# Equality matrices made in place from key rows that go through memory, no barrier after the first layer, and the second layer's totals from its scaled matrix

## The reference, cut to what matters

```python
edge_index = stack([src, dst])
x = layernorm(x + L0(x, edge_index))                    # two SAGE convolutions
x = layernorm(x + L1(x, edge_weight, src, dst))         # ten similarity-weighted steps
x = layernorm(x + L2(x, src, dst))                      # attention over edges, then an FFN
x = layernorm(x + L3(x, edge_attr_4, edge_attr_32, dst, src))  # equivariant messages

# L0, one convolution
agg = segment_sum(x[src], dst) / maximum(count(dst), 1)
y   = agg @ W_l.T + b_l + x @ W_r.T

# L1
xn  = x * rsqrt(maximum(sum(x * x, 1), 1e-12))
sim = where(src == dst, 0, sum(xn[src] * xn[dst], -1))
s   = exp(sigma)
sup = edge_weight * exp(sim / (2 * (2 * s * s)))
denom = b + segment_sum(sup, src) * a + a               # a = exp(alpha), b = exp(beta)
for _ in range(10):
    out = (x * b + (segment_sum(sup * out[dst], src) + out) * a) / denom
```

## Time and profile before

| | |
|---|---|
| time, median of 3 runs | 2785.97 us (2780.97 to 2790.19) |
| the profiled execution's own time | 2781.79 us |
| its span in the profile | 2780.0 us, mean granted TensorE clock 0.898 |
| busy | PE 82%, DVE 65%, POOL 41%, ACT 36% |
| barrier after the first layer's edge work | ends near 1303 us |
| PE matmuls, whole program | 9582 |

### The profile page before, as it was taken

How to read it: one execution, slowest core, us unless ns; L and a number is a source line. 1 busy time by engine, 2 the same in 40 slices (tenths; PEclk the granted TensorE clock), 3 DMA queues, 4 the chain that set the end, 5 groups by cost and what they waited for, 6 DMA issues and landing times.

```text
span 2780.0 us, 28864 instructions
## 1 busy us (share of the span) xinstructions
PE 2290.1 (82%) x9582; PEld 1197.5 (43%) x9582; DVE 1806.6 (65%) x3856; ACT 1008.9 (36%) x1735; POOL 1135.8 (41%) x869
## 2 busy tenths in 40 slices
PE   8999999999999689996076766739998898389786
PEld 4455555555555345453031211214444553254465
DVE  7999888888878861445753433544567658557753
ACT  2354545454555432210432322321121132265553
POOL 2766654455675724301645665620210201233222
PEclk9999999999999889998587988869999697599898
DMA  7333443333343435325744645670210202222221
GB/s 245 99 103 105 118 121 120 104 118 108 108 111 104 129 95 167 104 76 165 206 139 134 175 131 155 153 222 10 67 48 27 73 1 74 75 71 69 57 57 53
DMA packets 214547, 298.62 MB, mean 107 GB/s; under 512 B 100006, under 2 KB 100501, under 8 KB 213018
## 3 DMA queue, kind: packets, MB, share of 16 engines
q1 hardware_dynamic: 108186, 213.98, 25.7%
q0 software_dynamic: 106240, 83.12, 12.1%
HBM read 171.66 MB, written 160.65 MB: 120 GB/s over the span
## 4 chain that ended last, share of the span: by engine, by line
PE 56%; DVE 20%; issue 7%; POOL 6%; DMA 5%; ACT 5%; SPq 1%; POOLq 0%; DVEq 0%; ACTq 0%
PE bank L2031 8%; PE bank L320 8%; PE bank L1010 7%; PE bank L304 5%; POOL arena L1624 4%; PE bank L2627 3%; PE bank L296 3%; PE bank L990 2%; PE bank L311 2%; DMA arena<-y_table,ids 2%; DVE st L642 2%; POOL arena L1102 2%; PE bank L312 2%; PE bank L2510 2%; DMA x_table<-arena 2%
## 5 line engine op out<-in xcount | busy, mean ns | idle before, releaser
L1102 POOL DMA_INDIRECT arena<-x_table,idd x120 | 152.0, 1267 | 648.2 <-DVE arena L2297 157.1
L1678 PE MATMUL bank<-arena 125*125 125x512 f32 x360 | 207.5, 709 | 108.6 <-DMA arena<-y_table,ids 103.7
L2031 PE MATMUL bank<-arena 128*125 128x512 f32 x640 | 293.7, 614 | 1.4 <-DVE Md L2251 0.7
L304 PE MATMUL bank<-arena 128*125 128x512 f32 x640 | 285.2, 599 | 8.6 <-DMA ident<-ident_in 8.6
L1624 POOL DMA_INDIRECT arena<-y_table,ids x180 | 229.6, 1276 | 153.1 <-DMA y_table<-arena 101.0
L320 PE MATMUL bank<-arena 128*125 128x512 f32 x640 | 278.5, 593 | 2.1 <-ACT arena L517 1.8
L1852 DVE SCALAR_TENSOR_TENSOR arena<-arena,v,bank 125x512 f32<-125x512 f32 x180 | 134.3, 746 | 188.1 <-PE bank L1678 180.0
L811 POOL TENSOR_TENSOR arena<-arena,rowv 125x512 f32<-125x512 f32 x80 | 99.5, 1278 | 315.4 <-DVE arena L725 201.7
L1018 ACT ACTIVATE arena<-bank 128x500 f32<-128x500 f32 (+1 forms) x210 | 114.6, 589 | 279.3 <-PE bank L962 145.4
L1010 PE MATMUL bank<-arena 128*125 128x512 f32 x480 | 208.8, 593 | 0.0
L1729 ACT ACTIVATE bank<-arena 125x512 f32<-125x512 f32 x180 | 107.6, 600 | 267.5 <-DVE arena L1852 262.4
(11 more groups left out here) (404 smaller groups left out, 4417.4 us busy)
## 6 DMA issues: line engine op xcount, KB each, us to landing
y_table<-arena SPq DMA_DIRECT2D x36, 896.0 KB
p_table<-arena SPq DMA_DIRECT2D x25, 896.0 KB
z_table<-arena SPq DMA_DIRECT2D x25, 896.0 KB
x_table<-arena SPq DMA_DIRECT2D x25, 896.0 KB
arena<-x_cols SPq DMA_DIRECT2D x20, 1000.0 KB, 6.4
arena<-x SPq DMA_DIRECT2D x20, 896.0 KB
out<-arena SPq DMA_DIRECT2D x20, 896.0 KB
x_by_src<-arena SPq DMA_DIRECT2D x5, 896.0 KB
```

The costliest lines, as they stand in the source:

```text
L304: i = nc.tensor.matmul(b[0:P, :], xT[:, k, j * P:(j + 1) * P], W1r[:, k, :], start=k == 0, stop=k == KC - 1)
L1102: nc.gpsimd.indirect_dma_start(out=dst, out_offset=None, in_=table, in_offset=bass.IndirectOffsetOnAxis(ap=idx, axis=0), bounds_check=limi ...
L1678: nc.tensor.matmul(bank[t % RING1][0:P, :], Ss[:, t, :], V1[:, t, :], start=False, stop=True, skip_group_check=True).then_inc(P_sum, 1)
L2031: i = nc.tensor.matmul(b[0:P, :], fT[:, k, j * P:(j + 1) * P], W[:, k, :], start=k == 0, stop=k == KC - 1)
```

## The change

1. The hardware loop ends two steps earlier (LOOP_END 12 instead of 14), so all work on the records is done two steps earlier: DVE's in step 12, the scatters in 12 to 15, their return on SP in 15, DVE's part of it in 16.
2. A new table `key_rows` in memory holds the dst keys and the src keys as two rows of 2,500 numbers. When the scatters have landed, SP copies the key column of each record table into it (two DMAs from memory to memory, elements of 4 bytes that lie 192 bytes apart in the source), waits for both, and then loads the first row onto all 125 partitions of `Sd`. Only then it issues the loads that it issued before.
3. DVE makes `Sd` and `Md` in place from those key rows, in two parts, in steps 17 and 18 (BUILDS0), and the boundary weights in step 18. ACT's diagonals, PE's L1252 and DVE's reads of them from PSUM are gone, in both layers. SP's small transfers after the build move from step 20 to step 19.
4. `Ss` is loaded in the same way by SP near the end of the first layer's edge work, and made in place by DVE at the second layer's start.
5. The barrier `end_phase` is gone, and POOL does not wait for the build of `Ss` between its first gathers.
6. The second layer's scalars are in another order: what does not need ACT comes first, and the wait for ACT's exponential of the three parameters is parted from the wait for its root. `Ss` is scaled first, and PE takes the totals from the scaled matrix times a column of ones, four matmuls ahead of each group of `first_own`; DVE computes its ratio per group.

The diff, its core:

```diff
-        LOOP_START, LOOP_END = 8, NG - 6
+        LOOP_START, LOOP_END = 8, NG - 8
...
-            if isinstance(s, int) and s == BUILD0:
-                pe.wait_ge(NR_sb, st_.count("b_f", 4))
-                pe_build(pe, c, diag0, 1)
...
-            if isinstance(s, int) and s == BUILD0 - 1:
-                act.wait_ge(rec_done, 2)
-                for t in range(ET):
-                    i = nc.scalar.activation(diag0(t // TG)[:, t % TG, :], ident[0:P, 0:P], ACT.Identity,
-                                             scale=RD[:, t, Q_DST:Q_DST + 1])
-                i.then_inc(s_end, 1)
...
+            if isinstance(s, int) and s in BUILDS0:
+                dve_build(dve, c, 0, RD[:, :, Q_DST], Sd, Md, *BUILDS0[s])
+            if isinstance(s, int) and s == NG - 2:
+                link(dve, c, nc.vector.reciprocal(v20[:, 8, :], RD[:, :, Q_CNT]))
+                dve_boundary_weights(dve, c, Bd[:, :], 0, RD[:, :, Q_DST], None, bn0)
             if has(s, "S"):
                 finish(C, "sc", "rt", "rc", nS, 3)
-            if isinstance(s, int) and s == ENDS0:
-                link(dve, c, nc.vector.reciprocal(v20[:, 8, :], RD[:, :, Q_CNT]))
-                dve_boundary_weights(dve, c, Bd[:, :], 0, RD[:, :, Q_DST], None, bn0)
...
+        key_rows = nc.dram_tensor("key_rows", (2, E), F32).ap()
...
-        def end_phase(eng, c):
-
-            eng.drain().then_inc(phase_end, 1)
-            c.ph += 1
-            eng.wait_ge(phase_end, 4 * c.ph)
...
+        BUILDS0 = {LOOP_END + 5: (0, 3), LOOP_END + 6: (3, EG)}
...
             sv = RSd.rearrange("(t p) q -> p t q", p=P)
+            with nc.allow_non_contiguous_dma(reason="the keys of sorted records as two rows"):
+                sp.dma_start(key_rows[0], RDd[:, Q_DST]).then_inc(rec_back, 16)
+                sp.dma_start(key_rows[1], RSd[:, Q_SRC]).then_inc(rec_back, 16)
+            sp.wait_ge(rec_back, 16 * 2)
+            sp.dma_start(Sd, key_rows[0].rearrange("(t f) -> t f", f=P).partition_broadcast(P)).then_inc(rec_back, 16)
             sp.dma_start(RD[:, :, :], dv).then_inc(rec_back, 16)
             sp.dma_start(rec[:, :, :], sv).then_inc(rec_back, 16)
...
-        def dve_build(dve, c, q, key, S, M, dg):
-
+        def dve_build(dve, c, q, key, S, M, g0, g1):
+
+            t = slice(g0 * TG, g1 * TG)
             dve.wait_ge(dstep, c.d)
-            if dg is not None:
-                nc.vector.tensor_tensor(dg[:, :, :], spread(ident[0:P, 0:P], ET), b3(key, P),
-                                        ALU.mult).then_inc(s_end, 1)
-            for g in range(EG):
-                kt = gcols(key, g)
-                dve.wait_ge(R_ps, c.r + 1)
-                b = bank[4 + c.r % RN]
-                c.r += 1
-                row = b[0:P, 0:GR].rearrange("p (t f) -> p t f", f=P)
-                nc.vector.tensor_tensor(S[0:P, g * TG:(g + 1) * TG, :], row, b3(kt, P), ALU.is_equal)
-                nc.vector.tensor_copy(gcols(ck[:, q, 0:ET], g), row[:, :, 0])
-                i = nc.vector.tensor_copy(gcols(ck[:, q, ET:NB], g), row[:, :, P - 1])
-                if M is None:
-                    i.then_inc(R_sb, 1)
-                    continue
-                nc.vector.tensor_tensor(M[:, g * TG:(g + 1) * TG, :],
-                                        b[0:NB, 0:GR].rearrange("p (t f) -> p t f", f=P),
-                                        b3(gcols(bkm[:, q, :], g), P), ALU.is_equal).then_inc(R_sb, 1)
-            dve.wait_ge(R_sb, c.r)
-            link(dve, c, nc.vector.tensor_tensor(many[:, q, :], ck[:, q, 0:ET], ck[:, q, ET:NB], ALU.not_equal))
+            if M is not None:
+                nc.vector.tensor_tensor(M[:, t, :], S[0:NB, t, :], b3(bkm[:, q, t], P), ALU.is_equal)
+            nc.vector.tensor_copy(ck[:, q, t], S[:, t, 0])
+            link(dve, c, nc.vector.tensor_copy(ck[:, q, ET + g0 * TG:ET + g1 * TG], S[:, t, P - 1]))
+            i = nc.vector.tensor_tensor(S[:, t, :], S[:, t, :], b3(key[:, t], P), ALU.is_equal)
+            if g1 == EG:
+                link(dve, c, i)
+                link(dve, c, nc.vector.tensor_tensor(many[:, q, :], ck[:, q, 0:ET], ck[:, q, ET:NB], ALU.not_equal))
...
+            sp.wait_ge(R_sb, jobs0_done("z", EG - 1))
+            sp.dma_start(Ss, key_rows[1].rearrange("(t f) -> t f", f=P).partition_broadcast(P)).then_inc(rec_back, 16)
...
-        totals = bank[4][0:P, 0:ET]
-        totals_rdy, TOT0 = s_end, 2
+        totals = [bank[4 + 2 * (g % 2)][0:P, TG * g:TG * (g + 1)] for g in range(EG)]
...
             targets(0)
-            pool.wait_ge(R_sb, c.r + EG)
...
+            def group_totals(g):
+                pe.wait_ge(w1_rdy, g + 1)
+                if g >= 2:
+                    pe.wait_ge(P_raw, TG * (g - 1))
+                for j in range(TG):
+                    q = nc.tensor.matmul(totals[g][:, j:j + 1], Ss[:, TG * g + j, :], ones[:, 0:1], start=j == 0,
+                                         stop=True, skip_group_check=True)
+                q.then_inc(totals_rdy, 1)
...
             for g in range(EG):
                 tiles = range(TG * g, TG * (g + 1))
+                group_totals(g)
...
-            dve_build(dve, c, 1, RSs[:, :, 1], Ss, None, diag1)
+            dve.wait_ge(rec_back, 16 * 10)
+            dve_build(dve, c, 1, RSs[:, :, 1], Ss, None, 0, EG)
...
             nc.vector.tensor_scalar_max(v20[:, 5:7, :], v20[:, 5:7, :], 1e-12).then_inc(sc1, 1)
-            dve.wait_ge(sc1a, 2)
+            link(dve, c, nc.vector.tensor_tensor(TMP, RSs[:, :, 0], RSs[:, :, 1], ALU.not_equal))
+            link(dve, c, nc.vector.tensor_tensor(SD, SD, TMP, ALU.mult))
+            sg = v20[:, 8, 0:1]
+            dve.wait_ge(sc1a, 1)
             link(dve, c, nc.vector.reciprocal(v20[:, 5:7, :], v20[:, 5:7, :]))
             link(dve, c, nc.vector.tensor_tensor(SD, SD, SSQ, ALU.mult))
             link(dve, c, nc.vector.tensor_tensor(SD, SD, DSQ, ALU.mult))
-            link(dve, c, nc.vector.tensor_tensor(TMP, RSs[:, :, 0], RSs[:, :, 1], ALU.not_equal))
-            link(dve, c, nc.vector.tensor_tensor(SD, SD, TMP, ALU.mult))
-            sg = v20[:, 8, 0:1]
+            dve.wait_ge(sc1a, 2)
             link(dve, c, nc.vector.tensor_tensor(sg, abv[:, 2:3], abv[:, 2:3], ALU.mult))
             link(dve, c, nc.vector.tensor_scalar_mul(sg, sg, 4.0))
             link(dve, c, nc.vector.reciprocal(sg, sg))
             nc.vector.tensor_scalar(SD, SD, sg, None, ALU.mult).then_inc(sc1, 1)
             dve.wait_ge(sc1a, 3)
             al, be, both = abv[:, 0:1], abv[:, 1:2], v20[:, 9, 0:1]
-            nc.vector.tensor_tensor(both, al, be, ALU.add)
...
-            nc.vector.tensor_tensor(SUP, SD, RSs[:, :, 2], ALU.mult).then_inc(sc1, 1)
-            dve.wait_ge(sc1, 3)
+            link(dve, c, nc.vector.tensor_tensor(SUP, SD, RSs[:, :, 2], ALU.mult))
+
+            def scaled(g):
+                Sg = Ss[:, g * TG:(g + 1) * TG, :]
+                nc.vector.tensor_tensor(Sg, Sg, b3(gcols(SUP, g), P), ALU.mult).then_inc(w1_rdy, 1)
+            scaled(0)
             nc.vector.tensor_tensor(BM[:, :, 0:NM], BM[:, :, 0:NM], b3(SUP, NM), ALU.mult).then_inc(bm_rdy, 1)
-            for g in range(EG):
-                Sg = Ss[:, g * TG:(g + 1) * TG, :]
-                dve.wait_ge(totals_rdy, TOT0 + g + 1)
-                nc.vector.tensor_tensor(Sg, Sg, b3(gcols(SUP, g), P), ALU.mult).then_inc(w1_rdy, 1)
+            link(dve, c, nc.vector.tensor_tensor(both, al, be, ALU.add))
+            for g in range(1, EG):
+                scaled(g)
...
-            ratio(RR, NRR, totals, P)
             for t in range(ET):
+                if t % TG == 0:
+                    dve.wait_ge(totals_rdy, TOT0 + t // TG + 1)
+                    ratio(gcols(RR, t // TG), gcols(NRR, t // TG), totals[t // TG], P)
...
+                if isinstance(s, int) and s == NG - 1:
+                    sp.wait_ge(bn0, 1)
```

More of the change, by code:

```diff
@@ L415, in pe_step @@
                 rows_T("c_x", X3[par], True)
-            if isinstance(s, int) and s == BUILD0:
-                pe.wait_ge(R_sb, EG)
             if isinstance(s, int) and s == ENDS0:
@@ L1120, in scatter @@
                                          oob_is_err=False).then_inc(s, 16)
-        BUILD0, ENDS0, FIRST0 = NG, NG + 1, NG + 2
-        def diag0(g):
-            return at(GR * g if g < 4 else 34249, [TG, P], P)
+        ENDS0, FIRST0 = NG + 1, NG + 2
+        BUILDS0 = {LOOP_END + 5: (0, 3), LOOP_END + 6: (3, EG)}
         ones = sb("ones", [P, P])
@@ L1278, in gnn_kernel @@
             + [("n", g) for g in range(EG)]
-        R0 = EG
+        R0 = 0
         def jobs0_done(kind, g):
@@ L1647, in first_own @@
                                  stop=True).then_inc(P_sum, 1)
-            pe.wait_ge(sc1, 3)
-            for t in range(ET):
-                q = nc.tensor.matmul(totals[:, t:t + 1], Ss[:, t, :], SUP[:, t:t + 1], start=t == 0, stop=True,
-                                     skip_group_check=True)
-                if t % TG == TG - 1:
```

(4 more changed lines are left out.)

38 lines of the change are left out of this document (6 added, 32 removed).

## The result

The changed kernel takes 2805.41 us (median of 6 runs, 2798.88 to 2809.35), the kernel before 2787.76 us (6 runs, 2780.55 to 2795.06). The ratio is 1.0076, with a 95% interval of 1.0056 to 1.0095. The time lies within the forecast range, near the upper end, but the kernel became slower where no change was forecast as the likeliest. The condition of the third rival came, copies that take over 18 us (they took 22.9), and a time near its 2806. Its mechanism, small writes that are slow, did not (experiment 10), and the parts of its sum are not those measured, so that the near hit is in part luck.

The account below looks back on a forecast made before the run. PE's program order was taken as the bound. Second layer -13, drain -3, builds +1 and SP's queue +14.3 gave -0.7 on 2781.79, about 2781, or 2785 on the runs' scale; 8-in-10 range 2769 to 2806 us.

Parts of the forecast that it names:

- third rival: Node loop, SP's queue: 4-byte copies go at the pace of small writes, 30 us for both, total 2806; chance 0.18.
- term for SP's queue: Node loop, records' return: key copies and `Sd` load delay what is queued behind them, +14.3 us, ends +2.9 and +35.
- the prediction's own sign: Node loop: the prediction is wrong if no step is longer, or if one is longer by over 20 us.
- the copies: SP's queue: both key copies take 9.2 us, from 5.7 for the record loads plus 3.5; bounds 3.5 and 30.
- the load: SP's queue: loading 1250 KB into `Sd` takes 9.5 us at 135 GB/s, or 3.8 at 335 GB/s.
- the slack: Node loop: 4.4 us between the result store's read of its tile ending and DVE overwriting that tile, subtracted from the loss.
- The sum: Whole kernel: second layer -13, drain -3, builds +1, SP's queue +14.3, together -0.7 us against the profiled execution.
- Second layer's start: Second layer up to its first products: -10 until the products end, -1 table load, -2 totals, together -13 us.
- The landing of the last gather: Second layer's start: the last gather lands in 4 to 5 us instead of 10.78, a gain of 6.
- Drain: Node loop's steps 20 and 21: -1.9 and -1.9 us, +0.8 for a lower PE clock, together -3.
- Builds: DVE in steps 17 and 18: builds cost between 0 and 8.8 us, taken as +1.
- Rival 4: Second layer's totals: small groups with waits leave PE's clock low, up to 20 us more, 2805; chance 0.07.

Follow-up runs that it names:

- experiment 10: Changed kernel, with the records loaded first and the dst keys written to the key row from the loaded tile, not copied in memory: 2801.99 us, one execution.
- experiment 1: Changed kernel, with the src keys' copy moved to the first layer's edge work, so one key copy stands ahead of the `Sd` load: 2799.32 us, one execution.
- experiment 9: Changed kernel, with the `Sd` load cut into two DMAs of 112 and 13 partitions and nothing else: 2808.39 us, one execution.
- Experiment 6: Transfers spread over steps 15 to 17, builds in 17 and 18, barrier after the first layer back: ratio 1.0005 to the kernel before, 0.9974 without the barrier.
- experiment 7: Transfers spread over steps 15 to 17, builds in 17 and 18, totals as before the change: ratio 0.9989 to the kernel before, 0.9974 with grouped totals.
- experiment 4: Changed kernel, with record return, dst copy and `Sd` load spread over steps 15 to 17, builds in 18 and 19, src copy late: 2773.13 us, ratio 0.9958.

## Why the prediction failed

**The loss: mechanism and place right, size wrong.** The step that failed is the term for SP's queue, +14.3, where 32.2 came; 17.9 too little. By the prediction's own sign, a step longer by over 20 us, it was wrong: step 16 is 23.8 longer. The 17.9 have three parts.

- 13.7 are the copies: 22.9 us instead of 9.2. I took 5.7 us for 2,500 pieces from the record loads, which go from memory to SBUF, and let two run side by side. They do run side by side (the second adds 6.5), but one alone takes 16.4 (experiment 1), and from SBUF 7.9 (experiment 10): the nearest row had another kind of source and destination. It was also not a transfer's time: the 5.59 us of the earlier trace rows are how long SP's queue was held. The second key copy held it for only 4.80, and landed 21.94 us after its issue. The upper bound of 30 us held; my reason against it, that 1.49 is POOL's pace and not the DMA's, was not tested.
- 2.2 are the load: 11.7 beyond what the records took, against 9.5 (its own row, 135 GB/s, gives 9.3 for 1.25 MB, and 335 GB/s gives 3.7); 5.7 of them go when it is cut (experiment 9).
- 2.0 are the slack: I subtracted 4.4, where 34.6 us of delay on SP made 32.2 of stall, so 2.4.

The wait that I had named, DVE's for the result's store, is there; PE's for its columns, 24.73 us, stands beside it and was not in my sum. That freeing the result's tile earlier would have gained little follows from it, but no run tried it.

**The sum.** With 22.9 for the copies alone it gives -0.7 + 13.7 = +13, with the measured stall in the place of the whole term -0.7 + 17.9 = +17. That this meets the 17.6 of the medians is luck in part: in the two profiles the places that were forecast give 32.9 - 5.7 - 13.2 = +14.0, and the rest of their difference is elsewhere. The direction hung on one unknown price: the copies' bounds were 3.5 and 30 us, and I had taken 9.2, in the lowest quarter.

**Second layer's start: right in sum, one part by luck.** -13 forecast, -13.2 measured in this pair. The three profiles of the kernel before have 132.3 to 134.6 us for this stretch and ten with the change 121.3 to 124.4, so the gain is more nearly 10, with 8 and 13 as ends. By its parts, from the end of the first layer: first gather -2.6 (forecast -3.2), last gather's issue -7.9 (-7.8), products' end -9.3 (-10), start of the totals -9.9 (-11, or -10.4 with the scaling ahead of them), first products' end -13.2 (-13). The landing of the last gather failed: it gained 1.6 us and not 6, since its 9.15 us are near the 10.78 of before. The 4 us that I had taken off for squares and products hid that, so the -10 was right for a wrong reason. On PE the totals were to bring -2.6 to +0.6 (its own terms give -2.8). Experiment 6 gives 4 to 5 of the gain to the barrier, experiment 7 0.4 to 2 to the totals; the rest, the in-place build, POOL's freedom from it and the order of the scalars, was not undone alone.

**Drain: -5.7 in this pair against -3, and hardly told from nothing.** The two other profiles of the kernel before have 367.7 and 368.4 us for this stretch, the first 371.4; ten with the builds in steps 17 and 18 have 364.9 to 369.4. So the gain is some 2 us on the average, and the rest of the 5.7 is what two executions differ. In this pair PE's L296 of step 20 comes 2.7 us nearer to the last z store, the rest later; the 0.8 for a lower clock did not come (0.84 after, 0.80 before).

**Builds: right.** Step 19 is 0.7 longer than 45.5, step 18 not at all; +1 was forecast. Step 17 lies in the stall and can't be read. In experiment 4 no step shows them.

**Rival 4, the clock, did not come:** 1.00 from 1417 on, 6 us behind the first total.

**Not forecast: +6.2 at the start**, with the same instructions. See the last section; the cause stays open.

## What to carry to other kernels

A DMA that costs no engine anything still costs what is queued behind it: before adding one, list the transfers behind it on its queue and when their users want them, and put it where the queue has nothing urgent for as long as it runs. Here the same transfers cost 32 us in one step, and over three steps 4, or nothing with the builds a step later. Price a copy by the landing of one with the same source, destination and piece size, not by how long its issue held the queue; if there is none, the sign of a change that depends on it is open, and the forecast should say so. Two things are worth trying: to take small pieces from SBUF (7.9 us against 16.4 here), and to cut a load over 125 partitions in 112 and 13 (5.7 us sooner in its place). Neither showed in a time by itself. And before a difference of a few us in one pair of profiles is explained, look at the same stretch in a second profile of the same kernel: here the drain's 5.7 shrank to some 2.

## What the runs showed of the hardware

A copy of 2,500 elements of 4 bytes, 192 bytes apart, from memory to memory takes 14.8 to 16.4 us alone from its issue to that of the load that waits for it, a second one beside it 6.5 more; from SBUF 7.9 us.

In the first 50 us POOL's work slows DVE's. DVE counts keys in instructions of 0.35 us; when POOL runs 125 x 512 additions beside them, they take 1.23 to 1.45, as long as one addition (1.26). Changed kernel, DVE and POOL:

```profile
44.67 0.35 DVE L470 SCALAR_TENSOR_TENSOR Bd<-Md,kfc,ones 125x125 uint8<-125x125 f32 x1
...
46.53 1.23 DVE L470 SCALAR_TENSOR_TENSOR Bd<-Md,kfc,ones 125x125 uint8<-125x125 f32 x1
```

```profile
45.07 1.26 POOL L787 TENSOR_TENSOR arena<-arena,rowv 125x512 f32<-125x512 f32 x1 [13.66 <-DMA arena<-x]
```

In the first profile of the kernel before that addition starts at 46.98, 1.9 us later, and only one of the last DVE instructions meets it: 5 slow ones in all there, 6 in its second profile, 8 in each of twelve profiles with the change. That is the first 2.6 us of the 6.2. The start follows from the landing of a load of rows, whose instructions are the same. Three profiles without the change have the sixth z store at 257.8 to 260.4, twelve with it at 261.8 to 265.1; the unused table is not the reason, and what is stays open.
